# Attention and expert kernel: value sums moved to their rows by DMA and divided there, padded transpositions of maxima and expert weights

## Chip, cores, metric

One core of a Trainium2 chip. The metric is the device time of one execution, in microseconds; lower is better. Engines: PE (TensorE), DVE (VectorE), ACT (ScalarE), POOL (GpSimd), SP (SyncE, which here only issues DMAs).

## The reference

Two blocks over `x` of shape (2, 2048, 256). Block A is windowed attention with keys equal to values; block B is a rotary causal attention with 16 heads of 16, a gate, two of eight experts, and layer norms. Cut to what matters here:

```
x = layernorm(x + windowed_attention(x))                    # "a" steps
q = rope(x) @ Wq.T + bq ; k = rope(x) @ Wk.T + bk ; v = x @ Wv.T + bv      # "r" steps
attn = softmax(causal(q k^T / 4)) ; ctx = attn @ v          # jobs
x1 = LN(x + ctx @ Wo.T + bo) * w + b                        # "d" steps
gates = softmax(x1 @ gate_w.T + gate_b) ; top 2             # "f" steps
moe = sum over experts of gate_e * (x1 @ We.T + be)
x = layernorm(x + LN(x1 + moe) * w + b)                     # "g" steps
```

## The kernel before

The 4096 rows are 32 tiles of 128. Every tile passes the steps `a_*` (window attention), `r_*` (rotation, projections, split of q and k into three bf16 parts that are stored to DRAM and read back stacked) and later `d_*`, `f_*`, `g_*` (output projection, gate and experts, last norms). Between them lie 40 jobs, `JOBS[J] = (s, hg, j0, nj)`: group `s` of four tiles, head group `hg` of four heads, `nj` query tiles. In 24 full jobs `nj` is 4; the first and the last group are halved, 16 half jobs with `nj` = 2.

A job has two passes. First `mx` (PE, L1277) makes scores with queries on partitions and `mr` (DVE, L1006) reduces them to row maxima. `nm_a` to `nm_e` (DVE) negate them and split them into three bf16 parts, `nm_T` (PE, L1287) transposes them, tile by tile, `nm_Tc` (ACT, L900) copies them to `nmT`, and `nm_st` (SP, L749) sends them by four DMAs, one for each head, into three rows of `qs`, where they act as extra contraction rows. Then `st` (PE, L1307) makes the transposed scores with the maxima subtracted, `ex` (ACT, L920) exponentiates into `pbuf`, and `pv` (PE, L1329) sums values: four heads side by side in one bank, each with 16 value rows and a 17th row that holds the denominator. `st` of one job runs beside `mx` of the next.

At the end of a job `o_evac` (ACT) copies the bank to `osb`, `o_T` (PE, L1335) transposes it by tiles, `o_den` (DVE, L1048) inverts the denominators, `o_ctx` (DVE, L1058) multiplies into `ctxn`, which has query rows on partitions. For each tile `d_cT` (PE, L1411) transposes `ctxn` back, `d_cTc` (ACT) copies it, and `d_o` (PE, L1418) projects. In the expert part `f_wts` (DVE) is the row of eight weights, `f_wT` (PE, L1432) transposes it, `f_wTc` copies it, `f_b` (PE, L1435) multiplies it with the eight biases in fp32, and `f_e0` to `f_e3` (PE, L1440) are the experts' products.

All order is fixed beforehand: `plan()` runs a list schedule over the rows of `stage_steps()` and `job_steps()`, each with an engine, a cost in ns, a rank and what it waits for, and every engine executes its part of that one order in sequence. Seven PSUM banks are shared: at most three for `mx`, three for `st`, four for all other steps. A cost that is too low doesn't change the result, only where the engines wait.

Of the kernel before, what the change touches and what calls it, by code (L numbers as in the profile page):

```python
# [8 lines left out]
BF16 = mybir.dt.bfloat16  # L9
# [5 lines left out]
P = 128  # L15
# [7 lines left out]
GT = 4  # L23
# [9 lines left out]

STACKS = ((0, 0, 3, 0), (0, 3, 1, 0), (0, 4, 2, 0), (1, 0, 2, 0), (1, 2, 3, 0), (1, 5, 1, 0))
# [114 lines left out]
def late_count(T):  # L149
# [22 lines left out]
def stage_steps():  # L172
# [67 lines left out]
    for T in range(NT):  # L240
        l, tile = late_prior(T), LATE[T]
        alt = [("st0", NT - 1), ("r_vst", NT - 1), ("pst", NT - 1), ("pv_end", last_job(GB - 1))] if T > TAIL else []
        add("d_load", T, "SP", 450, ("st0", tile), ("d_res", l), *alt)
        add("d_xb", T, "POOL", 700, ("d_load", T), ("load_b2", 0))
        add("d_cT", T, "PE", 215, ("o_ctx", last_job(T // GT, T % GT)), ("d_o", l))
        add("d_cTc", T, "ACT", 280, ("d_cT", T))
        add("d_o", T, "PE", 860, ("d_cTc", T), ("d_aff", l), ("d_xb", T), ("load_moe", 0), ("load_ew", 0))
# [27 lines left out]
        add("f_e1", T, "PE", 1720, ("f_e0", T))  # L275
# [25 lines left out]
def job_steps():  # L301
# [8 lines left out]
    for J in range(NJ):  # L310
# [119 lines left out]
def build(nc, windows, cs, w_qk_t, w_out, in_t, in_b, wo_t, gate_t, exp_t, exp_b, rows, gate_b, out):  # L430
# [6 lines left out]
    with ExitStack() as ctx:  # L437
# [7 lines left out]
        small = sb("small", [P, 350])  # L445
# [96 lines left out]
        cT = [sb("cT", [P, EC, P])[:, :, :], qT[0], halves(room[4]), halves(room[5])]  # L542
        rD = [sb("rD", [P, E])[:, :], xb[0], room[6], room[7]]
# [12 lines left out]
        wT = [x[0:NE, 0:P] for x in accp]  # L556
# [36 lines left out]
        osb_ready, oden_ready = sem("osb_ready"), sem("oden_ready")  # L593

# [35 lines left out]
        CONSTS, MOE_LOADS = 12, 6  # L630
# [4 lines left out]
        def _(sp):  # L635
# [3 lines left out]
            for step in order:  # L639
# [852 lines left out]
```

## Time and profile before

| | |
|---|---|
| median of 3 runs | 1479.54 us (1478.23 to 1481.64) |
| profiled execution, time | 1473.93 us |
| profiled execution, span | 1472.1 us |
| instructions in the profile | 28143 |
| bytes read from HBM, written | 60.71 MB, 25.43 MB |

The span goes from the first to the last instruction of the profiled execution. Busy times are from the same execution; matmuls are pipelined and the end of each is modelled, so that the busy time of a short one contains a tail that the next one overlaps. The chain of work is followed back from the last instruction, at each step to what released it; its pieces go from start to start. A piece of idle time is put down to the semaphore that came last. "PEld" is the loading of weights, which runs beside the matmuls; "SPq" is SP's queue, which issues the DMAs.

### The profile page before, as it was taken

Reading aid. Unit: us, or ns where it says so; the run is one execution under the profiler, and the core shown is the slowest. Engines: PE = TensorE matmul, PEld = TensorE weight load, DVE = VectorE, ACT = ScalarE, POOL = GpSimd, SP = SyncE. Lnnn points to the kernel's source line nnn. Section 1 sums busy time; section 2 is a strip of 40 time slices with the busy share of each in tenths; the row PEclk is TensorE's granted clock in tenths of the full one; section 3 lists DMA queues with packets and bytes.
Section 4 is the critical chain, followed back from the end, with each engine's and each line's share of the span. In section 5 each row is a group of like instructions: output and inputs, shape, how many; then the busy total and the mean of one; then the engine's idle time right before and its main releaser. Section 6 shows DMA issues by size and latency. Waiting matters only on the chain.

```text
span 1472.1 us, 28143 instructions
## 1 busy us (share of the span) xinstructions
PE 1418.3 (96%) x9720; PEld 779.9 (53%) x9720; DVE 1080.3 (73%) x2604; ACT 800.2 (54%) x1707; POOL 427.8 (29%) x704
## 2 busy tenths in 40 slices
PE   8889999999999999999999999999999999999996
PEld 6757745555455545355556555555443345555442
DVE  3755877887788878787546777788777887878645
ACT  3235365555656566665654355555565566665641
POOL 4434423232322222221434433333211111011233
PEclk9999999999999999999999999999999999999998
DMA  3765522230222122010225232223110101111100
GB/s 117 187 172 120 132 56 56 56 88 24 59 56 56 43 61 56 24 45 24 53 68 112 70 87 68 55 57 80 27 48 14 25 24 24 33 31 30 29 26 15
DMA packets 150843, 88.60 MB, mean 60 GB/s; under 512 B 113902, under 2 KB 143862, under 8 KB 150447
## 3 DMA queue, kind: packets, MB, share of 16 engines
q1 hardware_dynamic: 150703, 86.80, 23.6%
q8 instruction: 79, 1.29, 0.4%
q14 instruction: 61, 0.50, 0.1%
HBM read 60.71 MB, written 25.43 MB: 59 GB/s over the span
## 4 chain that ended last, share of the span: by engine, by line
PE 82%; DMA 4%; SPq 4%; DVE 4%; issue 3%; ACT 2%; POOL 1%; POOLq 0%; DVEq 0%; ACTq 0%
PE bank L1329 16%; PE bank L1307 16%; PE bank L1440 14%; PE bank L1277 14%; SPq L749 4%; DMA qs<-eb_nmT 3%; PE bank L1399 3%; PE bank L1377 2%; PE bank L1385 2%; DVE mxs L1006 2%; PE bank L1360 2%; PE bank L1366 1%; PE bank L1405 1%; PE bank L1435 1%; PE bank L1281 1%
## 5 line engine op out<-in xcount | busy, mean ns | idle before, releaser
L1006 DVE TENSOR_REDUCE mxs<-bank 128x1 f32<-128x512 f32 (+3 forms) x1120 | 712.1, 667 | 186.7 <-PE bank L1277 122.0
L920 ACT ACTIVATE pbuf<-bank 128x512 f32<-128x512 f32 (+1 forms) x1112 | 592.2, 592 | 377.8 <-PE bank L1329 203.8
L1307 PE MATMUL bank<-qs,ks 99*128 99x256 bf16 (+3 forms) x1536 | 423.7, 319 | 19.5 <-DMA qs<-eb_nmT 19.3
L1277 PE MATMUL bank<-ks,qs 96*128 96x512 bf16 (+3 forms) x1280 | 421.7, 349 | 2.2 <-DVE mxs L1006 1.7
L1329 PE MATMUL bank<-pbuf,vcur 128*17 128x256 f32 (+3 forms) x3072 | 271.4, 471 | 2.1 <-ACT pbuf L920 1.5
L1307 PEld LDWEIGHTS bank<-qs,ks 99*128 99x128 bf16 x1536 | 140.1, 98 | 199.3 <-issue 112.1
L1440 PE MATMUL bank<-ew,x1T 128*128 128x512 f32 x464 | 220.7, 597 | 0.0
L1277 PEld LDWEIGHTS bank<-ks,qs 96*128 96x128 bf16 x1280 | 123.7, 99 | 126.1 <-issue 52.8
L1329 PEld LDWEIGHTS bank<-pbuf,vcur 128*17 128x17 f32 x3072 | 70.7, 96 | 144.5 <-issue 104.1
L1440 PEld LDWEIGHTS bank<-ew,x1T 128*128 128x128 f32 x464 | 84.2, 190 | 69.0 <-issue 56.9
L900 ACT ACTIVATE etmp<-bank,small 128x256 f32<-128x256 f32 x116 | 48.6, 470 | 78.8 <-PE bank L1440 78.8
L869 POOL TENSOR_TENSOR accp<-accp,etmp 128x256 f32<-128x256 f32 x29 | 21.0, 725 | 223.9 <-ACT etmp L900 223.9
L1281 PE MATMUL bank<-maskb,idb 128*128 128x128 bf16 x384 | 81.1, 220 | 0.0
L865 POOL TENSOR_TENSOR accp<-etmp 128x256 f32<-128x256 f32 x29 | 21.1, 728 | 181.2 <-ACT etmp L900 181.2
L1312 PE MATMUL bank<-idb,maskb 128*128 128x128 bf16 x352 | 73.8, 220 | 0.0
L1203 DVE SCALAR_TENSOR_TENSOR acc<-bank,small,acc 128x256 f32<-128x256 f32 x58 | 28.1, 484 | 54.3 <-PE bank L1440 54.0
L1399 PE MATMUL bank<-rxT,inw 128*128 128x128 f32 x464 | 57.1, 276 | 0.0
L1399 PEld LDWEIGHTS bank<-rxT,inw 128*128 128x128 f32 x464 | 55.4, 192 | 2.0 <-issue 1.0
L815 POOL TENSOR_SCALAR small<-small 128x1 f32<-128x1 f32 x32 | 7.1, 221 | 165.9 <-DVE small L1082 165.9
L841 POOL CAST parts<-qkf 128x512 bf16<-128x512 f32 x28 | 17.3, 618 | 120.2 <-DVE qkf L1098 120.2
L900 ACT ACTIVATE qT<-bank 128x256 f32<-128x256 f32 x59 | 22.7, 384 | 36.8 <-PE bank L1377 19.7
L1281 PEld LDWEIGHTS bank<-maskb,idb 128*128 128x128 bf16 x384 | 37.7, 98 | 8.2 <-issue 3.3
(267 smaller groups left out, 1761.3 us busy)
## 6 DMA issues: line engine op xcount, KB each, us to landing
vcur<-v_scratch SPq DMA_DIRECT2D x92, 136.0 KB, 2.4
parts_scratch<-parts SPq DMA_DIRECT2D x29, 384.0 KB, 3.3
xw<-windows SPq DMA_DIRECT2D x29, 256.0 KB, 2.9
qs<-parts_scratch SPq DMA_DIRECT2D x32, 192.0 KB, 3.4
ks<-parts_scratch SPq DMA_DIRECT2D x32, 192.0 KB, 3.6
ks<-parts_scratch SPq DMA_DIRECT2D x32, 128.0 KB, 2.9
qs<-parts_scratch SPq DMA_DIRECT2D x32, 128.0 KB, 3.5
v_scratch<-vst SPq DMA_DIRECT2D x29, 136.0 KB, 2.1
```

The costliest lines, as they stand in the source:

```text
L749: sp.dma_start(qs5[KR:KR + NPART, place(J) % QRING, j0:j0 + nj, hg * HJ + h, :], nmT[h * NPART:(h + 1) * NPART, 0:nj * P].rearrange("p (j ...
L900: return nc.scalar.activation(o, i, ACT.Copy, scale=scale)
L920: nc.scalar.activation(pbuf[:, u0:u0 + heads, nj * P - cols:nj * P], bk[:, 0:heads * cols].rearrange("p (h t) -> p h t", h=heads), ACT.Exp)\
L1006: v.reduce_max(mxs[:, j * HJ + h:j * HJ + h + heads, c], bk[:, 0:heads * cols].rearrange("p (h t) -> p h t", h=heads), AX_X)\
L1277: last = mm(bk[:, x * cols:(x + 1) * cols].rearrange("p (n t) -> p n t", t=P), qs5[0:KR, pos % QRING, j, head, :], ks5[0:KR, kslot, 0:cols ...
L1281: last = mm(bk[:, x * cols + j * P:x * cols + (j + 1) * P], idb[:, :], maskb[:, :], start=False, stop=True)
L1307: last = mm(bk[:, x * cols:(x + 1) * cols].rearrange("p (n t) -> p n t", t=P), ks5[0:KR + NPART, kslot, kb % GT, head, :], qs5[0:KR + NPAR ...
L1312: last = mm(bk[:, x * cols:x * cols + P], maskb[:, :], idb[:, :], start=False, stop=True)
L1329: last = mm(obank[32 * h:32 * h + DV, r0:r1], vcur[:, kb, h, :], pbuf[:, (kb * HJ + h) % PB, r0:r1], start=kb == 0, stop=kb == nk - 1, til ...
L1360: last = mm(bk[:, co * P:(co + 1) * P], m_sb[:, ci, co * P:(co + 1) * P], xT[e][:, ci, P:2 * P], start=ci == 0, stop=ci == EC - 1)
L1399: last = mm(bk[:, co * P:(co + 1) * P], inw[:, ci, co * P:(co + 1) * P], rxT[e][:, ci, :], start=ci == 0, stop=ci == EC - 1)
L1440: last = mm(bk[:, :], x1T[f][:, c, :], ew[:, c, k * 2 * E:(k + 1) * 2 * E], start=c == 0, stop=c == EC - 1)
```

## The change

Value sums: `o_T`, `o_den`, `o_ctx`, `d_cT` and `d_cTc` are gone. `o_mv` (SP) waits for `osb` and issues five DMAs within SBUF: one for each head, 16 rows of `osb` to the rows of `ctxT` that `d_o` contracts over, and one that copies the four denominator rows to the 16 rows of their head in `oden`. After each second job of a group (`hg` 1 and 3) `o_rec` (DVE) inverts the 128 rows of `oden` and `o_nrm` (POOL) multiplies the part of `ctxT` in place. `d_o` reads `ctxT` directly. `rD` is now the tile `x0b`, so `d_load` waits for `d_aff` of the tile before in place of `d_res`.

Maxima: `nmp` is one 128x128 bf16 tile, zero beyond the parts, transposed by one instruction; `nm_Tc` copies 128 columns; `nm_st` issues one DMA for each tile in place of one for each head.

Expert biases: `f_wp` to `f_ws` (DVE) split the weights into three bf16 parts and lay them out in six slots of a padded tile, which `f_wT` transposes in bf16; `ebp` holds the biases in bf16 parts for the same slots (made once by `w_eb`, and `load_ebp`, six DMAs), and `f_b` is one bf16 product. `f_e0` no longer waits for `f_b`, `f_e1` does.

Cut to its core:

```diff
@@ stage_steps
+    add("w_eb", 0, "DVE", 1200, ("load_moe", 0))
+    add("load_ebp", 0, "SP", 2700, ("w_eb", 0))
...
-        add("d_load", T, "SP", 450, ("st0", tile), ("d_res", l), *alt)
+        add("d_load", T, "SP", 450, ("st0", tile), ("d_aff", l), *alt)
-        add("d_cT", T, "PE", 215, ("o_ctx", last_job(T // GT, T % GT)), ("d_o", l))
-        add("d_cTc", T, "ACT", 280, ("d_cT", T))
-        add("d_o", T, "PE", 860, ("d_cTc", T), ("d_aff", l), ("d_xb", T), ("load_moe", 0), ("load_ew", 0))
+        add("d_o", T, "PE", 860, ("o_nrm", last_job(T // GT, T % GT)), ("d_xb", T), ("load_moe", 0), ("load_ew", 0))
...
+        add("f_wp", T, "DVE", 100, ("f_wts", T), ("f_wT", T - 1))
+        add("f_wq", T, "DVE", 100, ("f_wp", T))
+        add("f_wr", T, "DVE", 100, ("f_wq", T))
+        add("f_ws", T, "DVE", 100, ("f_wr", T))
+        add("f_wT", T, "PE", 100, ("f_ws", T), ("f_b", l), ("f_es", l))
+        add("f_wTc", T, "ACT", 200, ("f_wT", T), ("f_es", l))
+        add("f_b", T, "PE", 200, ("f_wTc", T), ("load_ebp", 0))
-        add("f_e0", T, "PE", 1720, ("f_b", T))
+        add("f_e0", T, "PE", 1720, ("d_x1Tc", T))
@@ job_steps
-        add("nm_T", J, "PE", 420, r - 1, ("nm_e", J))
-        add("nm_Tc", J, "ACT", 495, r - 1, ("nm_T", J), ("nm_st", J - 1))
-        add("nm_st", J, "SP", 1600, r - 1, ("nm_Tc", J))
+        add("nm_T", J, "PE", 100, r - 1, ("nm_e", J))
+        add("nm_Tc", J, "ACT", 200, r - 1, ("nm_T", J), ("nm_st", J - 1))
+        add("nm_st", J, "SP", 1300, r - 1, ("nm_Tc", J))
...
-        add("o_evac", J, "ACT", 495, r + length / 2, ("pv", J, nk - 1), ("o_T", J - 1))
-        add("o_T", J, "PE", 440, r + length / 2, ("o_evac", J), ("d_cT", freed))
-        add("o_den", J, "DVE", 120, r + length / 2, ("o_T", J))
-        add("o_ctx", J, "DVE", 340, r + length / 2, ("o_den", J), ("d_cT", freed))
+        add("o_evac", J, "ACT", 495, r + length / 2, ("pv", J, nk - 1), ("o_mv", J - 1))
+        add("o_mv", J, "SP", 2200, r + length / 2, ("o_evac", J), ("d_o", freed), ("o_nrm", J - 1 - hg % 2))
+        if hg % 2:
+            add("o_rec", J, "DVE", 55 + nj * 133, r + length / 2, ("o_mv", J))
+            add("o_nrm", J, "POOL", 300 + nj * 214, r + length / 2, ("o_rec", J))
@@ SP
+                    for j in range(nj):
+                        sp.dma_start(qs5[KR:KR + NPART, place(J) % QRING, j0 + j, hg * HJ:(hg + 1) * HJ, :],
+                                     nmT[j * NPART * HJ:(j + 1) * NPART * HJ, :]).then_inc(nm_loaded, 16)
+                elif name == "o_mv":
...
+                    sp.wait_ge(osb_ready, J + 1)
...
+                    to = hg % 2 * HJ * DH
                     for h in range(HJ):
+                        sp.dma_start(ctxT[to + h * DH:to + (h + 1) * DH, pos % 2, hg // 2, j0 * P:(j0 + nj) * P],
+                                     osb[32 * h:32 * h + DH, 0:nj * P]).then_inc(ctx_loaded, 16)
+                    sp.dma_start(oden[to:to + HJ * DH, 0:nj * P],
+                                 osb[DH:P:32, 0:nj * P].unsqueeze(1).broadcast_to([HJ, DH, nj * P])).then_inc(ctx_loaded, 16)
@@ POOL
+            for m in (ebp, wpad, nmp):
+                pool.memset(m[:, :], 0.0).then_inc(consts, 1)
+                elif name == "o_nrm":
...
+                    pool.wait_ge(ctx_loaded, 80 * (T + 1))
+                    pool.wait_ge(oden_ready, T // 2 + 1)
+                    pool.tensor_tensor(part, part, oden[:, 0:nj * P], ALU.mult).then_inc(ctx_ready, 1)
@@ DVE
+                    dve.wait_ge(ctx_loaded, 80 * (T + 1))
+                    v.reciprocal(oden[:, 0:nj * P], oden[:, 0:nj * P]).then_inc(oden_ready, 1)
@@ PE
+                    tr(bk[:, 0:P // 2].bitcast(BF16), nmp[:, :], idb[:, :]).then_inc(filled[b], 1)
...
-                    pe.wait_ge(*drain("d_cT", T))
+                    pe.wait_ge(ctx_ready, (last_job(T // GT, T % GT) + 1) // 2)
...
-                    tr(bk[0:NE, 0:P], wts[f], idf[:, :]).then_inc(filled[b], 1)
+                    tr(bk[:, 0:P // 2].bitcast(BF16), wpad[:, :], idb[:, :]).then_inc(filled[b], 1)
...
-                    mm(bk[:, 0:E], wT[f], eb, start=True, stop=True).then_inc(filled[b], 1)
+                    mm(bk[:, 0:E], wT[f], ebp[:, :], start=True, stop=True).then_inc(filled[b], 1)
```

## Rows read from the trace of the kernel before

**Rows 1.** The page, busy us, share of the span and instructions of each engine.
```profile
PE 1418.3 (96%) x9720; PEld 779.9 (53%) x9720; DVE 1080.3 (73%) x2604; ACT 800.2 (54%) x1707; POOL 427.8 (29%) x704
```

**Rows 2.** The page, shares of the chain that ended last, by engine.
```profile
PE 82%; DMA 4%; SPq 4%; DVE 4%; issue 3%; ACT 2%; POOL 1%; POOLq 0%; DVEq 0%; ACTq 0%
```

**Rows 3.** Waits of PE: us in total, times, longest us.
```profile
PE bank L1307 <- DMA qs<-eb_nmT: 19.3, 22, 4.6
...
PE bank L1277 <- DVE mxs L1006: 1.7, 6, 0.5
```

**Rows 4.** Waits of DVE's reductions for PE.
```profile
DVE mxs L1006 <- PE bank L1277: 122.0, 117, 3.6
...
DVE mxs L1006 <- PE bank L1281: 62.9, 60, 4.0
```

**Rows 5.** Chain in order of time, 629 to 660 us: start, us, what.
```profile
631.65 0.32 PE bank L1287 x4
631.97 0.59 PE bank L1335 x4
...
632.77 0.22 PE bank L1411 x2
...
637.51 0.22 PE bank L1277
...
655.50 0.62 PE bank L1435 x2
```

**Rows 6.** Groups by form on DVE: count, busy us, mean ns, idle before.
```profile
L1006 DVE TENSOR_REDUCE mxs<-bank 128x1 f32<-128x512 f32 x896 | 582.0, 682 | 139.9 <-PE bank L1277 112.8 <-PE bank L1281 26.2
...
L1058 DVE TENSOR_TENSOR ctxn<-bank,oden 128x256 f32<-128x256 f32 x24 | 10.0, 415 | 0.0
...
L1048 DVE RECIPROCAL oden<-bank 128x16 f32<-128x16 f32 x24 | 6.0, 252 | 0.5 <-PE bank L1335 0.3
...
L1163 DVE RECIPROCAL small<-small 128x1 f32<-128x1 f32 x32 | 5.0, 158 | 1.2 <-ACT small L972 0.7
...
L1048 DVE RECIPROCAL oden<-bank 128x8 f32<-128x8 f32 x16 | 3.2, 201 | 3.1 <-PE bank L1335 3.1
```

**Rows 7.** Timeline, boundary of two jobs near 1106 us: start, us, instruction, idle.
```profile
1105.38 0.60 ACT L900 ACTIVATE osb<-bank 128x512 f32<-128x512 f32 x1 [0.34 <-PE bank L1329]
1106.57 0.59 ACT L900 ACTIVATE eb_nmT<-bank 12x512 bf16<-12x512 bf16 x1 [0.30 <-PE bank L1287]
1107.19 3.00 SPq L749 DMA_DIRECT2D qs<-eb_nmT  x4
1111.38 0.47 PE L1307 MATMUL bank<-qs,ks 99*128 99x512 bf16 x1 [2.96 <-DMA qs<-eb_nmT]
```

**Rows 8.** Timeline, ACT and SP at a boundary near 632 us.
```profile
630.97 0.58 ACT L900 ACTIVATE osb<-bank 128x512 f32<-128x512 f32 x1
631.00 0.37 SPq L741 DMA_DIRECT2D vcur<-v_scratch  x1
632.92 3.01 SPq L749 DMA_DIRECT2D qs<-eb_nmT  x4
```

**Rows 9.** The page, DMA issues: KB each, median us from issue to landing.
```profile
parts_scratch<-parts SPq DMA_DIRECT2D x29, 384.0 KB, 3.3
...
x0b<-x_scratch SPq DMA_DIRECT2D x29, 128.0 KB, 2.1
```

**Rows 10.** Windows: us, then PE, PEld, DVE, ACT, POOL busy, PEclk, DMA share, GB/s.
```profile
1111.50:1114.90 3.40, 3.40 (x9) 0.99 (x7) 2.30 (x4) 2.28 (x5) 0.00 (x0) 0.50 0.00 0
```

**Rows 11.** Groups by form on ACT: the copy of 128 columns.
```profile
L900 ACT ACTIVATE accp<-bank 8x128 f32<-8x128 f32 x29 | 7.5, 257 | 4.9 <-PE bank L1432 4.9
```

**Rows 12.** Timeline, end of the last job and the projection behind it.
```profile
1422.89 0.38 ACT L900 ACTIVATE osb<-bank 128x256 f32<-128x256 f32 x1 [1.89 <-PE bank L1329]
...
1428.45 1.03 PE L1418 MATMUL bank<-wo,ks 128*128 128x256 f32 x4
```

More of the change, by code:

```diff
@@ L114, in st_last, with tiles_before @@
     return max(i for i, x in enumerate(st_list(J)) if x[0] <= kb)
+def tiles_before(J):
+    return sum(x[3] for x in JOBS[:J])
 def loads_before(J, c):
@@ L159 @@
 EMPTIES = {"w_m": "w_mc", "w_o": "w_oc", "a_xT": "a_xTc", "a_q": "a_qc", "a_s": "a_exp", "a_pT": "a_pTc", "a_y": "a_yc", "a_o": "a_res", "r_rT": "r_rTc",
-           "r_qk": "r_qkf", "r_v": "r_vst", "nm_T": "nm_Tc", "d_cT": "d_cTc", "d_o": "d_res", "d_x1T": "d_x1Tc",
+           "r_qk": "r_qkf", "r_v": "r_vst", "nm_T": "nm_Tc", "d_o": "d_res", "d_x1T": "d_x1Tc",
            "f_g": "f_lg", "f_wT": "f_wTc", "f_b": "f_acc0", "f_e0": "f_e0c", "f_e1": "f_e1c", "f_e2": "f_e2c",
-           "f_e3": "f_e3c", "o_T": "o_ctx", "mx": "mr", "st": "ex"}
+           "f_e3": "f_e3c", "mx": "mr", "st": "ex"}
 EMPTIED_FOR = {reader: filler for filler, reader in EMPTIES.items()}
@@ L467, in build @@
         ew = sb("ew", [P, EC, NE * E])
-        eb_nmT = sb("eb_nmT", [2 * 32, E])
-        eb = eb_nmT[0:NE, :]
-        nmT = eb_nmT[32:32 + NPART * HJ, :].bitcast(BF16)
+        ebp = sb("ebp", [P, E], BF16)
+        wpad = sb("wpad", [P, P], BF16)
         qkb = sb("qkb", [P, 2 * EC])
@@ L541, in build @@
         x0f = [sb("x0f", [P, E])[:, :], xw[0][:, 1, :], room[2], room[3]]
-        cT = [sb("cT", [P, EC, P])[:, :, :], qT[0], halves(room[4]), halves(room[5])]
-        rD = [sb("rD", [P, E])[:, :], xb[0], room[6], room[7]]
+        rD = x0b
         x1 = [sb("x1", [P, E])[:, :], x0[0], room[8], room[9]]
@@ L1019, in _ @@
                     nj = JOBS[T][3]
-                    whole = nm[:, 0:nj * HJ].rearrange("p (j h) -> p j h", j=nj)
-                    rest = nmd[:, 0:nj * HJ].rearrange("p (j h) -> p j h", j=nj)
-                    part = [nmp[:, 0:nj, :, a] for a in range(NPART)]
+                    whole, rest = (x[:, 0:nj * HJ].rearrange("p (j h) -> p j h", j=nj) for x in (nm, nmd))
+                    part = [nmp[:, 0:nj * NPART * HJ].rearrange("p (j a h) -> p j a h", j=nj, a=NPART)[:, :, a, :]
+                            for a in range(NPART)]
                     if name == "nm_b":
+                        if T == 0:
+                            dve.wait_ge(consts, CONSTS)
                         if T:
@@ L1285, in _ @@
                     pe.wait_ge(nmp_ready, T + 1)
-                    for j in range(JOBS[T][3]):
-                        last = tr(bk[0:NPART * HJ, 0:GQ // 2].bitcast(BF16)[:, j * P:(j + 1) * P], nmp[:, j, :, :].rearrange("p h a -> p (h a)"), idb[:, :])
-                    last.then_inc(filled[b], 1)
+                    tr(bk[:, 0:P // 2].bitcast(BF16), nmp[:, :], idb[:, :]).then_inc(filled[b], 1)
                 elif name == "st":
@@ L1331, in _ @@
                     last.then_inc(pv_done, 1)
-                elif name == "o_T":
-                    pe.wait_ge(osb_ready, T + 1)
-                    for j in range(JOBS[T][3]):
-                        last = tr(bk[:, j * P:(j + 1) * P], osb[:, j * P:(j + 1) * P], idf[:, :])
-                    last.then_inc(filled[b], 1)
                 elif name in ("w_m", "w_o"):
@@ L1407, in _ @@
                     last.then_inc(filled[b], 1)
-                elif name == "d_cT":
-                    pe.wait_ge(*drain("o_T", last_job(T // GT, T % GT)))
-                    for c in range(EC):
-                        last = tr(bk[:, c * P:(c + 1) * P], ctxn[:, T % (2 * GT), c * P:(c + 1) * P], idf[:, :])
-                    last.then_inc(filled[b], 1)
                 elif name == "d_o":
```

117 lines of the change are left out of this document (76 added, 41 removed).

## Prediction

> **What bounds the kernel now.** I read the page first, then the waits, the chain in order of time, the groups by form, and the timeline where one job ends and the next begins. PE is busy for 1418.3 of 1472.1 us, DVE for 73% of the span, ACT for 54% [rows 1]. The chain that ended last is 82% PE; DMA, SP's issuing and DVE have 4% each [rows 2]. PE's named waits are few: 19.3 us in 22 waits for the maxima to land in `qs` (`nm_st`), 1.7 us for DVE's reductions [rows 3]. So PE's program is the path, and a microsecond taken from it counts, as long as the other engines deliver in time. Two things say how well they do. DVE idles 1.04 us in the mean before a reduction that waits for PE (122.0 us in 117 times, 62.9 in 60) [rows 4]: it follows PE closely, and a pause of DVE much longer than that is felt by PE. And PE executes an order that `plan()` fixed from the costs written in the kernel; where a real step is longer than its planned one, PE stands at the next instruction that needs it.
>
> The profiled execution has a span of 1472.1 us and a time of 1473.93; the median of the three runs is 1479.54, 0.4% above. I work out a difference on the span and add it to the median.
>
> **Part 1, PE work removed.** A busy mean of a short matmul contains its pipeline's tail, so I price by the chain, which goes from start to start [rows 5]. `o_T`: four transpositions 0.59 us in each of 24 full jobs, half of that in 16 half jobs, 19.0 us. `d_cT`: 0.22 x 32 tiles = 7.0. `nm_T`: four in 0.32 become one in 0.08, 24 x 0.24 + 16 x 0.08 = 7.0. `f_b`: two passes of an 8-row fp32 product in 0.62 become one bf16 product of 256 columns; a bf16 product of 512 columns takes 0.22 there, so I take 0.11 and get 0.51 x 32 = 16.3; at 0.22 it is 12.8. `f_wT` in bf16: one `d_cT` piece takes 0.11, one `nm_T` piece 0.08, 0.03 x 32 = 1. Sum 46.8 to 50.3, I take **-47 us**. The evacuations that go with them (`cT`, the longer copy of `nmT`) relieve ACT, which isn't the bound: nothing.
>
> **Part 2, the division.** Before, DVE inverts 16 numbers per partition (252 ns) or 8 (201) and multiplies from PSUM (415 for a full job) [rows 6]: 24 x 0.667 + 16 x some 0.5 = 24 us. After, `o_rec` inverts denominators that were copied to all 16 rows of a head: 512 columns 12 times, 256 columns 8 times. No row has a wide reciprocal. One column costs 158 ns, 8 cost 201, 16 cost 252: 6.4 ns per column from 8 to 16. A reduction passes 512 columns in 682 ns [rows 6], which is the lower bound, 0.7 us. The slope gives 0.25 + 496 x 0.0064 = 3.4 us, and 1.8 us for 256 columns. I take the slope, as it is the same operation; its two points are strided reads of PSUM, which keeps the lower bound open. DVE's sum: 12 x 3.4 + 8 x 1.8 = 55, plus 4 x 32 `f_wp` to `f_ws` at 0.2 = 26, plus 2 for `w_eb`, less 24: **+59 us of DVE**, 77% busy. That alone wouldn't bound.
>
> The place does. The plan prices `o_rec` at 55 + 133 per tile, 587 ns; with 3.4 us DVE is 2.8 us late, and with it what is queued behind: the reductions `mr` that empty the banks of `mx` (three at most), residuals and sums of the layer norms, the gates. The transfers add to it. `o_mv` is five SP instructions. A plain load takes 0.37 us to issue [rows 8], those of `nm_st`, over three partitions, 0.75 (3.00 for four) [rows 7]. Bounds 1.9 and 3.75 us for five; four of the five span 16 partitions, so I take 2.3. Landing: 2.1 us for 128 KB, 3.3 for 384 KB [rows 9]; the broadcast writes 128 KB from 4 source rows, and I take 3. From the end of `o_evac` to `o_rec` that makes 5.3 us where the plan has 4.1, 1 us late. Full job: 1.0 + 2.8 - 1.04 of slack = 2.8 us of PE idle, 12 times **+34** (bounds: 0 if the reciprocal is cheap and the data are in time; 12 x 4.5 = 54 at the dear issue and landing). Half job: 1.5 + 0.3 late, little above the slack, 8 x 0.5 = **+4** (0 to 12). `o_nrm`, `d_rstd` behind it on POOL and `d_o` on PE stand in the same pause as the reductions, so they aren't priced apart.
>
> What the Trainium skill adds stands apart: "VectorE: DVE Perf Modes", section "First, the fixed hardware budget", says that the reciprocal is an iterative divide with a repeat count of 8. With the 0.96 GHz that the same page of the Trainium skill has under "Specifications" this is, as an estimate, 8.3 ns per column and 4.3 us for 512, and the sum would be 12 x 0.9 = 11 us dearer. The slope of [rows 6] is nearer to it than to one column per cycle.
>
> **Part 3, the maxima.** The copy `nm_Tc` comes down from about 0.6 towards the 257 ns of a 128-column copy [rows 11], `nm_T` by 0.24. `nm_st` of a full job still has four DMAs over three partitions, 3.0 us; that of a half job has two in place of four, 1.5 us less. Where `st` starts some 1.2 us behind the last issue (1107.19 + 3.00 to 1111.38 [rows 7]) this is on the path. By the timeline I count four half jobs of that kind, 4 x 1.8, **-7**, and six full ones with no `o_mv` near, 6 x 0.6, **-4**. In 15 full jobs, though, the sums of the job before are evacuated 0.6 to 2.4 us ahead of `nm_st`: `osb` ends at 1105.98, `nm_st` starts at 1107.19 [rows 7]; 631.55 and 632.92 [rows 8]. There `o_mv` gets into SP's queue first, and `nm_st` and the loads of keys, queries and values stand behind it. 1107.19 becomes 1105.98 + 0.1 + 2.3 = 1108.4, 1.2 us later than now. Part is planned (2200 ns stands in the table) and filled with other work, part isn't: from -0.6 (if `nm_st` goes first) to 2.7, I take 1.0; 15 x 1.0 = **+15**.
>
> **Part 4, the clock.** Before 1111.38 PE stood 2.96 us for `nm_st` [rows 7]; right after, the granted clock was 0.50, 1.2 GHz, for 3.4 us [rows 10]. Half of 3.4, 1.7 us, is lost by such a fall. New pauses of that length will bring some: I take five, **+8** (0 to 15 x 1.7 = 26).
>
> **Part 5, edges.** Start: three more memsets on POOL of the size of those that stand beside the first loads, nothing. Six small DMAs of `ebp` at 0.75 and `w_eb`, while SP issues the loads of the first jobs: 0 to 5, **+2**. End: the last `o_mv`, `o_rec` and `o_nrm` need 0.1 + 2.3 + 2.6 + 1.8 + 0.1 + 0.7 = 7.6 us from 1423.3, so `d_o` starts near 1430.9 and not 1428.45 [rows 12], +2.4; `f_e0`, which no longer waits for `f_b`, gives some back: **+1**. `x0b` serving as `rD` lets `d_load` start some 3 us later, once per tile, and tiles lie 10 us and more apart: nothing. DVE's 26 us of `f_wp` to `f_ws` lie behind `f_wts`, beside expert products; in an engine that is 27% idle they make 0 to 8, **+3**.
>
> **Sum.** -47 + 34 + 4 - 7 - 4 + 15 + 8 + 2 + 1 + 3 = +9 us: 1479.5 + 9 = **1488**.
>
> **Rivals.** (a) The forecast: pauses of DVE and SP eat the gain of PE and more. 0.46; its own range is 1482 to 1502. (b) Faster: PE's removed work counts and the pauses are hidden, by a wide reciprocal near the 0.7 us bound or by work that PE doesn't need soon. Then -47 - 11 + 16 for what remains of the pauses, + 12 for the rest: -30, 1450. For it: PE has 82% of the chain and lost only 1.7 us to DVE. Against: the slope, and 1.04 us of slack. It decides for a pause below some 1.5 us. 0.25. (c) The two cancel, -12 to +2: 1468 to 1482. 0.20. (d) SP's queue bounds every boundary: `nm_st` 2.7 us late in 15 places (+25 against my term) and a fall of the clock at most of them (+18), not all of it together: 1512. It decides when `o_mv` takes 3.75 us to issue. 0.09.
>
> Faster by over 0.2% (3 us, about what a measurement of this kernel tells from no change): (b) and half of (c), 0.35. Within: 0.12. Slower: 0.53. Both signs hold much. The range for 8 in 10 is 1453 to 1510; it leaves out the lower half of (b) and part of (d).
>
> **What would show it.** In the profile after: a reciprocal of 128x512 near 3.4 us (0.7 turns me to (b), 4.3 to the skill's estimate); PE's waits for DVE's `mxs` up from 1.7 to 20 us or more, with PE's idle before `d_o` beside them; the wait for `qs` above 19.3; four DMAs of `o_mv` at 0.4 and one at 0.75 to issue; a mean granted clock under the present one. I am wrong in kind if PE's idle time grows by less than 40 us, and wrong in size if the new order of `plan()`, which the trace of before can't show, puts `o_rec` where DVE has room.

## The result and the profile after

The change makes the kernel slower than every case I had written down: 1604.47 us (1604.04 to 1606.6) against 1479.23, a ratio of 1.0847, 95% interval 1.0828 to 1.0866, +125 us. I had forecast 1488 and a range to 1510. The profiled execution has a span of 1602.5 us, 130.4 above the one before.

The page of the changed kernel, busy time of each engine and the line of the granted clock in 40 slices, answers to [rows 1]:

```profile
PE 1433.8 (89%) x9408; PEld 766.4 (48%) x9408; DVE 1138.2 (71%) x2676; ACT 776.8 (48%) x1675; POOL 452.4 (28%) x727
...
PEclk9988999999999989999999999999998999999997
```

PE has 312 instructions fewer and is yet busy for 15.5 us longer, while its share fell from 96% to 89%; DVE's fell from 73% to 71% though it has 58 us more to do. Idle time has come in on both engines, and PE's work itself has slowed down. PE's waits by what they waited for (us in total, times, longest), answer to [rows 3]:

```profile
PE bank L1373 <- DMA qs<-nmT: 46.8, 17, 6.1
PE bank L1474 <- POOL ctxT L896: 32.1, 6, 8.7
PE bank L1354 <- DVE nmp L1084: 15.2, 4, 7.2
PE bank L1345 <- DVE mxs L1052: 11.5, 11, 5.7
PE bank L1373 <- DVE mxs L1052: 7.0, 14, 1.8
```

L1373 is `st`, L1474 `d_o`, L1354 `nm_T`, L1345 `mx`. The wait for the maxima to land grew from 19.3 to 46.8 us. `d_o` now waits for `o_nrm`, `nm_T` for the split maxima, `mx` for the reductions: 64 us more than before, in few and long pieces. Next, DVE's own waits, answer to [rows 4]. Those of its reductions for PE grew by 13 us in all; the new row behind them is its stand at `o_rec`:

```profile
DVE mxs L1052 <- PE bank L1345: 123.4, 111, 3.2
DVE mxs L1052 <- PE bank L1349: 74.7, 64, 3.4
DVE oden L1095 <- DMA oden<-osb: 57.7, 19, 6.0
```

The groups by form (busy us, mean ns, idle before), answer to [rows 6] and [rows 11]: the wide reciprocal, what POOL waits for behind it, two of the four steps of the padded weights (290 to 166 ns, 25.7 us in all four), and the short copy of the maxima.

```profile
L1095 DVE RECIPROCAL oden<-oden 128x512 f32<-128x512 f32 x12 | 40.2, 3353 | 37.8 <-DMA oden<-osb 37.8
L896 POOL TENSOR_TENSOR ctxT<-ctxT,oden 128x512 f32<-128x512 f32 x12 | 15.2, 1265 | 89.0 <-DVE oden L1095 89.0
L1095 DVE RECIPROCAL oden<-oden 128x256 f32<-128x256 f32 x8 | 14.0, 1752 | 20.0 <-DMA oden<-osb 20.0
...
L1245 DVE TENSOR_TENSOR small<-small,wpad 128x8 f32<-128x8 f32 x32 | 9.3, 290 | 0.2
...
L1249 DVE TENSOR_TENSOR wpad<-small,wpad 128x8 bf16<-128x8 f32 x32 | 5.3, 166 | 0.1
...
L948 ACT ACTIVATE nmT<-bank 48x128 bf16<-48x128 bf16 x24 | 6.4, 266 | 19.5 <-PE bank L1354 19.4
```

One boundary shows how the pieces hang together. Timeline of the changed kernel, end of job 27 (start, us, instruction, idle before), answer to [rows 7]; it is put together from the rows of five engines, in order of time:

```profile
1101.80 0.60 ACT L948 ACTIVATE osb<-bank 128x512 f32<-128x512 f32 x1 [1.17 <-PE bank L1395]
...
1103.78 2.48 SPq L788 DMA_DIRECT2D ctxT<-osb  x4
1106.31 0.64 SPq L790 DMA_DIRECT2D oden<-osb  x1
1107.06 1.59 SPq L749 DMA_DIRECT2D qs<-parts_scratch  x2
...
1109.66 3.07 SPq L774 DMA_DIRECT2D qs<-nmT  x4
1110.77 3.35 DVE L1095 RECIPROCAL oden<-oden 128x512 f32<-128x512 f32 x1 [3.23 <-DMA oden<-osb]
1114.26 1.27 POOL L896 TENSOR_TENSOR ctxT<-ctxT,oden 128x512 f32<-128x512 f32 x1 [9.84 <-DVE oden L1095]
1115.67 2.04 PE L1474 MATMUL bank<-wo,ctxT 128*128 128x256 f32 x4 [6.00 <-POOL ctxT L896]
1117.51 0.63 PE L1373 MATMUL bank<-qs,ks 99*128 99x512 bf16 x1
```

`osb` is full at 1102.4, `o_mv` starts 1.4 us later and takes SP's queue 3.2 us, its last transfer lands 3.8 us after that. DVE stands 3.23 us at `o_rec` and then divides for 3.35; POOL multiplies for 1.27; PE stands 6.00 us before `d_o`. `nm_st` starts at 1109.66, behind two loads and a store that stand before it in SP's order. From the full `osb` to `d_o` it is 13.3 us. The windows of the same boundary (us, busy of PE, PEld, DVE, ACT, POOL, granted clock, DMA), and of two other places, answer to [rows 10]:

```profile
1106.00:1112.80 6.80, 3.67 (x28) 3.06 (x26) 3.51 (x6) 0.54 (x2) 0.00 (x0) 1.00 0.33 88
1112.90:1119.60 6.70, 3.93 (x9) 2.64 (x10) 5.89 (x13) 1.73 (x4) 4.74 (x5) 0.50 0.12 40
1119.70:1126.00 6.30, 6.05 (x37) 2.16 (x36) 4.59 (x11) 4.14 (x9) 1.48 (x3) 1.00 0.41 107
1215.30:1228.80 13.50, 8.15 (x24) 1.84 (x28) 11.36 (x18) 4.67 (x8) 1.95 (x2) 0.50 0.08 24
```

While PE stands, the granted clock falls to 0.50 (1.2 GHz) at 1112.8 and stays there until 1119.6, over `d_o` (four products in 2.04 us, where four took 1.03 at the full clock [rows 12]) and the first `st` of the next job. The fourth row is 13.5 us at half clock, with PE busy for 8.15 of them; they begin within a pause of 6.1 (the longest of the wait for `qs`). The chain of this profile covers only some 40% of the span, so its shares, unlike [rows 2], tell nothing.

For the whole execution I laid the trace's records of the granted clock against PE's idle pieces. The time lost to the clock is half of what PE works at 0.50; what it idles there is counted once, as idle. The idle time includes the 4 us before PE's first instruction.

| | span | PE idle | at half clock (spells) | of it PE idle | lost to the clock | rest |
|---|---|---|---|---|---|---|
| before | 1472.1 | 43.0 | 26.1 (5) | 3.7 | 11.2 | 1418.0 |
| after | 1602.5 | 157.8 | 175.7 (24) | 44.3 | 65.7 | 1379.1 |

The 130.4 us are +114.8 of idle, +54.5 of slow clock and -38.9 of work removed. The rest is the span less the idle time and less what the clock lost: what the kernel would take if PE never stood and the clock never fell. As a remainder it holds the errors of the others: the six kernels of the table of mended prices have the same instructions and rests from 1372.8 to 1389.8, so a difference of rests is good to some 17 us and no better. Spans are of the profiled executions; that of before is a short one (1473.93 us of time against medians of 1477.6 to 1479.5, a mean granted clock of 0.991 where the other executions have 0.984 to 0.992), so differences of spans and of medians differ by up to 5 us, and part of the +54.5 belongs to that choice.

The end, answer to [rows 12]: timeline of the last job and the projection behind it.

```profile
1556.93 0.38 ACT L948 ACTIVATE osb<-bank 128x256 f32<-128x256 f32 x1 [0.96 <-PE bank L1395]
...
1562.85 1.75 DVE L1095 RECIPROCAL oden<-oden 128x256 f32<-128x256 f32 x1 [5.96 <-DMA oden<-osb]
...
1565.61 3.75 PE L1474 MATMUL bank<-wo,ctxT 128*128 128x256 f32 x8 [8.74 <-POOL ctxT L896]
```

### The profile page after: what moved, and what is told of

The parts are those of the page before. It is cut to its first block and busy times, and to the rows that moved or that the text cites. A ratio compares the mean times of both kernels' runs of the same rounds, so it can differ in the third digit from the quotient of the medians.

```text
span 1602.5 us, 27748 instructions
## 1 busy us (share of the span) xinstructions
PE 1433.8 (89%) x9408; PEld 766.4 (48%) x9408; DVE 1138.2 (71%) x2676; ACT 776.8 (48%) x1675; POOL 452.4 (28%) x727
## 5 line engine op out<-in xcount | busy, mean ns | idle before, releaser
L1373 PE MATMUL bank<-qs,ks 99*128 99x256 bf16 (+3 forms) x1536 | 441.3, 332 | 58.4 <-DMA qs<-nmT 46.8
L1345 PE MATMUL bank<-ks,qs 96*128 96x512 bf16 (+3 forms) x1280 | 436.1, 361 | 14.5 <-DVE mxs L1052 11.5
L1373 PEld LDWEIGHTS bank<-qs,ks 99*128 99x128 bf16 x1536 | 143.3, 100 | 258.4 <-issue 150.3
L1345 PEld LDWEIGHTS bank<-ks,qs 96*128 96x128 bf16 x1280 | 126.2, 101 | 154.2 <-issue 56.8
L1095 DVE RECIPROCAL oden<-oden 128x512 f32<-128x512 f32 (+1 forms) x20 | 54.2, 2712 | 57.7 <-DMA oden<-osb 57.7
L1474 PE MATMUL bank<-wo,ctxT 128*128 128x256 f32 x128 | 40.8, 451 | 32.1 <-POOL ctxT L896 32.1
L901 POOL TENSOR_TENSOR x0b<-x0b,rowv 128x256 f32<-128x256 f32 x29 | 21.1, 728 | 149.9 <-DMA x0b<-x_scratch 148.6
L896 POOL TENSOR_TENSOR ctxT<-ctxT,oden 128x512 f32<-128x512 f32 (+1 forms) x20 | 21.0, 1052 | 137.4 <-DVE oden L1095 137.4
```

The lines of the kernel that those rows point to most:

```text
L1095: v.reciprocal(oden[:, 0:nj * P], oden[:, 0:nj * P]).then_inc(oden_ready, 1)
L1345: last = mm(bk[:, x * cols:(x + 1) * cols].rearrange("p (n t) -> p n t", t=P), qs5[0:KR, pos % QRING, j, head, :], ks5[0:KR, kslot, 0:cols ...
L1373: last = mm(bk[:, x * cols:(x + 1) * cols].rearrange("p (n t) -> p n t", t=P), ks5[0:KR + NPART, kslot, kb % GT, head, :], qs5[0:KR + NPAR ...
L1474: last = mm(bk[:, 0:E], ctxT[:, T // GT % 2, c, T % GT * P:(T % GT + 1) * P], wo[:, c, :], start=c == 0, stop=c == EC - 1)
```

## The experiments

My theory after the result: neither the instructions nor the transfers are what costs 125 us, but the order that `plan()` makes from prices that are too low. `o_mv` stands there at 2200 ns and with the default size of 4 KB for its landing, `o_rec` at 55 + 133 per tile, `nm_st` at 1300. The rivals: the reciprocal's length as such; the queue of SP as such; the clock, started by any pause. Times of before in the tables are those of runs on the same chip.

### Each half alone

The pads alone: `nm_T`, `nm_st`, `f_wp` to `f_b` and `ebp` as in the change, the value sums as before. The value sums alone: `o_mv`, `o_rec`, `o_nrm`, `d_o` as in the change, the maxima and the biases as before.

> The padded maxima and the bf16 expert biases alone; value sums go through PE's two transpositions as before. Theory A (the time is lost in the value sums' transfers and the wide reciprocal): about 25 us faster than the kernel before, 1445 to 1465, as PE loses 0.51 x 32 for the biases and 7 us of maxima transpositions, and nm_st of half jobs gets shorter. Rival B (the small DVE steps f_wp to f_ws and the new order cost as well): 1475 to 1500.

> The value sums by transfers alone; maxima and biases as before. Theory A: all of the loss and more is here, 1610 to 1640. Rival B (loss shared by both parts, or only through their meeting): 1540 to 1590.

| | us | before | ratio (95%) | idle | lost to the clock | rest |
|---|---|---|---|---|---|---|
| pads alone | 1464.58 | 1478.24 | 0.9917 (0.9888 to 0.9947) | 46.8 | 15.7 | 1400.2 |
| value sums alone | 1625.59 | 1478.24 | 1.1009 (1.0973 to 1.1045) | 152.3 | 72.4 | 1397.8 |

The loss lies in the value sums: +147 us, and the pads take 13.7 off. The sum, +134, is near the +125 of both together. Both numbers are those of theory A, though its "about 25 us" for the pads was nearly twice what came. The rests put PE's removed work at -17.8 for the pads and -20.2 for the value sums, with the error named above.

PE's waits in the kernel with the value sums alone:

```profile
PE bank L1313 <- DMA qs<-eb_nmT: 36.4, 16, 4.0
PE bank L1428 <- DVE small L1197: 20.4, 7, 9.2
PE bank L1283 <- DVE mxs L1024: 18.3, 15, 6.0
```

The same stall of DVE at `o_rec` comes out at other places of PE's program: here L1428, the transposition of the gate weights (`f_wT`), which in the changed kernel hardly waits. Which step is the victim is a matter of the order; that there is one isn't.

### The reciprocal without its time

The changed kernel with a multiplication by 1.0 in the reciprocal's place; the division of the value sums is left out.

```diff
-                    v.reciprocal(oden[:, 0:nj * P], oden[:, 0:nj * P]).then_inc(oden_ready, 1)
+                    v.tensor_scalar(oden[:, 0:nj * P], oden[:, 0:nj * P], 1.0, None, ALU.mult).then_inc(oden_ready, 1)
```

> The changed kernel with a multiplication by 1.0 in place of the reciprocal of oden, so the division is left out; order and all waits as in the changed kernel. It takes 12 x 2.7 + 8 x 1.3 = 43 us from DVE. Theory A1 (the length of the reciprocal is the main cost): DVE's pauses shrink from some 6 us to 3.5, falls of the clock become few, 1604 goes to 1500 to 1540. Rival A2 (DVE standing for the landing of oden, SP's queue ahead of nm_st, and the clock falls behind these are the main cost): 1560 to 1590, with PE's wait for qs still over 40 us.

1559.85 us, ratio 1.0556 (1.0514 to 1.0598): 44.6 us below the changed kernel. 81 us of the 125 stay. The time lies at the very edge of theory A2, 20 us from A1. The groups by form and the waits of this kernel:

```profile
L1095 DVE TENSOR_SCALAR oden<-oden 128x512 f32<-128x512 f32 x12 | 5.4, 448 | 38.5 <-DMA oden<-osb 38.5
...
PE bank L1373 <- DMA qs<-nmT: 46.8, 17, 5.5
PE bank L1474 <- POOL ctxT L896: 19.9, 6, 7.3
PE bank L1354 <- DVE nmp L1084: 8.4, 4, 3.9
```

DVE works 46.1 us less at this place and PE idles 34.6 us less, at `d_o`, `nm_T` and `mx` above all, and loses 6 us less to the clock. DVE's stand for the transfer (38.5 us in the full jobs, 37.8 before) and PE's wait for `qs` don't move.

### The plan told the truth

Five kernels have the changed kernel's instructions and other prices. One has all of these, the others one or two:

```diff
-          "load_moe": 300, "load_ew": 2048, "st0": 128, "vstore": 136, "pst": 384, "d_load": 128, "g_load": 128,
+          "load_moe": 300, "o_mv": 400, "load_ew": 2048, "st0": 128, "vstore": 136, "pst": 384, "d_load": 128, "g_load": 128,
...
-        add("nm_st", J, "SP", 1300, r - 1, ("nm_Tc", J))
+        add("nm_st", J, "SP", nj * 750, r - 1, ("nm_Tc", J))
...
-        add("o_mv", J, "SP", 2200, r + length / 2, ("o_evac", J), ("d_o", freed), ("o_nrm", J - 1 - hg % 2))
+        add("o_mv", J, "SP", 3150, r + length / 2, ("o_evac", J), ("d_o", freed), ("o_nrm", J - 1 - hg % 2))
...
-            add("o_rec", J, "DVE", 55 + nj * 133, r + length / 2, ("o_mv", J))
+            add("o_rec", J, "DVE", 55 + nj * 825, r + length / 2, ("o_mv", J))
```

400 KB is no size that is moved; at the plan's 5 ns per KB it is 2.0 us more of landing. `plan()` lets transfers pass one after another, so this number also sets back the transfers that it places behind `o_mv`.

> The changed kernel with four costs in the plan set to what its trace shows (o_mv 3150 and a landing longer by 2 us, nm_st 750 per tile, o_rec 55 + 825 per tile); the work is the same, only the order moves. Theory C (the loss comes from a plan that doesn't know the real lengths): 1604 goes to 1480 to 1530 and the granted clock comes back to 0.98 or more. Rival D (the lengths themselves hurt, no order hides them): 1560 to 1610.

> The changed kernel with only o_rec's cost set right in the plan (55 + 825 per tile in place of 133). C1: 20 to 40 us back, 1565 to 1585. C2: 60 or more, under 1545.

> The changed kernel with only o_mv's cost set right in the plan (3150 and a landing longer by 2 us). Of the 115 us that all four costs gave back: theory C1 (the steps wait for each other in one pause, and knowing where it begins is worth most) 60 to 90 us, 1515 to 1545. Rival C2 (the reciprocal's price is what matters): under 40 us, 1565 or more.

> The changed kernel with one number of the plan altered: the issuing of o_mv is priced at 3150 ns in place of 2200. The pair of prices for o_mv (issue 3150 and 400 KB for its landing) had brought 1604 to 1519 us. Theory I (the SP queue: nm_st and the loads stand behind an o_mv that takes 0.95 us longer than planned): most of the 85 us come from this number, 1535 to 1560 us here, and the wait for qs falls from 46.8 to near 23 us while DVE's wait for oden stays near 50. Theory L (the landing, which the plan has at zero size, so that DVE stands at o_rec): this number gives back little, 1580 to 1600 us, and DVE's wait for oden stays above 50 us.

> The changed kernel with the other number alone: o_mv enters the plan as a transfer of 400 KB, so that o_rec is placed behind its landing; its issuing stays at 2200 ns. Theory I: 1575 to 1600 us, the wait for qs stays above 40 us. Theory L: 1520 to 1545 us, DVE's wait for oden falls from 57.7 to under 20 us and PE's waits for the reductions' mxs below 8 us.

| prices mended | us | before | ratio (95%) | idle | lost to the clock | rest |
|---|---|---|---|---|---|---|
| none | 1604.47 | 1479.23 | 1.0847 (1.0828 to 1.0866) | 157.8 | 65.7 | 1379.1 |
| `o_rec` | 1573.68 | 1479.52 | 1.0644 (1.0601 to 1.0688) | 130.6 | 64.0 | 1381.1 |
| `o_mv`, issue | 1575.28 | 1477.55 | 1.0664 (1.0637 to 1.0691) | 134.1 | 61.0 | 1377.3 |
| `o_mv`, landing | 1560.82 | 1477.55 | 1.0566 (1.0534 to 1.0597) | 119.1 | 69.6 | 1372.8 |
| `o_mv`, both | 1518.88 | 1479.52 | 1.0274 (1.0237 to 1.031) | 94.0 | 33.8 | 1387.0 |
| all | 1489.55 | 1478.24 | 1.0081 (1.0053 to 1.011) | 71.6 | 29.0 | 1389.8 |

115 of the 125 us come back with four numbers changed and not one instruction, as theory C had it. This is the finding of the case. Its parts: 85.6 us by the pair for `o_mv` and 30.8 by the price of `o_rec`, both as C1 had them; the price of `nm_st` wasn't tried alone in this kernel. The pair isn't one of its halves: issue alone gives 29, landing alone 44, together less than both at once. Neither of theories I and L has its number. The landing is what makes DVE stand: its wait for `oden` falls from 57.7 to 18.9 us with the landing priced, to 41.1 with the issue. But the wait for `qs` moves with neither alone (45.0 and 44.2), only with both (22.9), and the clock's loss likewise; with `o_rec` priced alone it rises to 58.0. And PE's waits for the reductions, which L had below 8 us, are 31.8 with the landing priced: what leaves one place comes out at another. Waits with the landing priced alone:

```profile
PE bank L1373 <- DMA qs<-nmT: 44.2, 20, 4.7
PE bank L1373 <- DVE mxs L1052: 22.0, 15, 3.6
PE bank L1345 <- DVE mxs L1052: 9.8, 18, 3.4
```

Waits with all prices mended:

```profile
PE bank L1373 <- DMA qs<-nmT: 18.0, 16, 3.5
PE bank L1474 <- POOL ctxT L896: 5.9, 3, 4.8
...
DVE oden L1095 <- DMA oden<-osb: 11.3, 7, 4.5
```

And the boundary of job 27 in that kernel, rows of SP, DVE, POOL and PE in order of time, with its window:

```profile
1014.64 2.49 SPq L788 DMA_DIRECT2D ctxT<-osb  x4
1017.17 0.64 SPq L790 DMA_DIRECT2D oden<-osb  x1
...
1018.34 3.54 SPq L774 DMA_DIRECT2D qs<-nmT  x4
1021.53 3.35 DVE L1095 RECIPROCAL oden<-oden 128x512 f32<-128x512 f32 x1
...
1025.03 1.27 POOL L896 TENSOR_TENSOR ctxT<-ctxT,oden 128x512 f32<-128x512 f32 x1 [1.29 <-DVE oden L1095]
1026.45 1.10 PE L1474 MATMUL bank<-wo,ctxT 128*128 128x256 f32 x4
```

```profile
1013.00:1030.00 17.00, 16.33 (x89) 10.53 (x87) 16.53 (x45) 7.76 (x19) 6.32 (x8) 1.00 0.56 145
```

The transfers take as long as in the changed kernel (3.2 us to issue, 3.7 until `o_rec`), the reciprocal takes 3.35 us, the multiplication 1.27. PE and DVE hardly stand: DVE is busy for 16.5 of 17 us, PE for 16.3, the clock is 1.00.

One rival isn't excluded by a run of its own: that some of the gain is due to another order as such and not to the right one. No order from prices altered at random was run. Against it stands that each of the five price changes here made the kernel faster, and the two of `nm_st` below didn't make theirs slower.

### The clock by itself

The changed kernel with additional products whose result is overwritten: 10 before the first `st` of each job and 20 before `d_o` of seven tiles, so that PE works where it would stand.

```diff
+                        for _ in range(10):
+                            mm(bk[:, :].rearrange("p (h t) -> p h t", h=HJ), maskb[:, :],
+                               idb[:, :].unsqueeze(1).broadcast_to([P, HJ, P]), start=True, stop=True)
```

> The changed kernel, its plan and waits as they are, with extra products on PE ahead of two of its waits: 10 of 512 columns (2.2 us) before each first st of a job, 20 (4.4 us) before d_o of seven tiles, written to a bank that the real products overwrite. They add work and take the idle time away. Theory E (each pause costs twice, by itself and by the 3.4 to 7 us of half clock behind it; 178 us at half clock in the changed kernel, 28 before): half-clock time falls under 100 us and the time to 1545 to 1580, although PE has more to do. Rival F (the clock's falls come from elsewhere or cost little): 1604 to 1650, as 40 x 2.2 us of work are added where the wait is shorter.

1635.56 us, ratio 1.1063 (1.1029 to 1.1097), 31 us slower. Idle is 96.3 (-61.5), lost to the clock 44.1 (-21.6), the rest 1493.3 (+114.2, the 540 products). The groups of the added products:

```profile
L1367 PE MATMUL bank<-idb,maskb 128*128 128x512 bf16 x400 | 95.0, 385 | 0.5 <-DVE mxs L1052 0.5
...
L1477 PE MATMUL bank<-idb,maskb 128*128 128x512 bf16 x140 | 37.7, 433 | 4.4 <-DVE mxs L1052 4.4
```

The time is that of rival F and not of theory E (1545 to 1580). F's reason, that the falls come from elsewhere, isn't borne out: the time at half clock fell from 175.7 to 100.1 us. Of the 114.2 us added, 61.5 took the place of standing; the other 53 made the kernel longer and cost more than the clock gave back. The run agrees with the share that I give the clock (21.6 us of slow clock go with 61.5 us of idle, 0.35 per us; with all prices mended it was 36.7 with 86.2, 0.43) and doesn't prove it: it isn't a run in which the clock alone was changed, and there is none.

### What is left over

The kernel with all prices mended, 1490 us, stands above the pads alone. Three more runs ask what its value sums still cost, and how much of the pads' gain is a price as well.

```diff
-            add("o_rec", J, "DVE", 55 + nj * 825, r + length / 2, ("o_mv", J))
+            for k in range(nj):
+                add(f"o_rec{k}", J, "DVE", 60 + 825, r + length / 2, ("o_mv", J), *[(f"o_rec{k - 1}", J)] * (k > 0))
...
-                    v.reciprocal(oden[:, 0:nj * P], oden[:, 0:nj * P]).then_inc(oden_ready, 1)
+                    k = int(name[5:])
+                    v.reciprocal(oden[:, k * P:(k + 1) * P], oden[:, k * P:(k + 1) * P]).then_inc(oden_ready, 1)
```

> The kernel with the plan priced by the trace (1490 us), and o_rec cut into pieces of 128 columns, four of some 0.9 us in place of one of 3.35, each a step of its own, so that reductions can stand between them. Theory P (what is left of the loss is the unbroken pause of DVE): PE's gaps fall from 71.6 to near 60 us and the time to 1470 to 1480. Theory Q (the plan already puts the reciprocal where DVE has room, and what is left is the work and the order): 1485 to 1497, DVE's work only 3 us more.

1493.0 us, 1.0122 (1.0092 to 1.0153): no gain, as theory Q had it; the 3 us more lie within the two intervals. Idle is 75.9 (71.6 unsplit), and the 64 pieces take DVE 59.7 us where the 20 wide ones took 54.1. In this kernel, a pause that the plan knows needn't be cut.

> The kernel with the plan priced by the trace (1490 us), with the reciprocal of the denominators replaced by a multiplication by 1.0 (the division is left out), and priced as what it takes: 55 + 75 ns per tile in place of 55 + 825. It removes some 46 us of DVE's work from a kernel whose plan knows it. The pads with nm_st at its price stand at 1462.5 without the transfers, 27 us lower. Theory R (what the transfer route still costs is the wide reciprocal): 1462 to 1474 us. Theory S (it is the transfers: SP's 3.1 us in front of nm_st and their landing before d_o): 1480 to 1490 us, the wait for qs stays near 18 us.

1482.09 us, 1.0026 (1.001 to 1.0042): 7.5 us below the 1489.55 of the kernel with its reciprocal, as theory S had it (the ratios differ by 0.0055, and their intervals just don't meet). The same edit took 44.6 us off where the plan had the price wrong. So 46 us of DVE's work cost 45 us unplanned, and 44 us of it cost 7 planned. Some 20 of the 27 us over the pads with `nm_st` priced (below) stay, and lie with the transfers or the order around them: idle is 70.9 against 44.1, the clock loses 21.4 against 12.4, the wait for `qs` is 15.2 against 3.6, and `d_o` waits 10.2. Which of SP's queue and the landing holds them is open.

```diff
-        add("nm_st", J, "SP", 1600, r - 1, ("nm_Tc", J))
+        add("nm_st", J, "SP", 3000, r - 1, ("nm_Tc", J))
```

This edit is of the kernel before; in the pads alone the same price became `nj * 750`.

> The kernel before the change with nothing altered but the plan's price of nm_st, 3000 ns (what the trace shows for its four DMAs) in place of 1600. Theory W (the wait for qs, 19.3 us and the falls of the clock behind it, is a price that the plan has wrong, in the kernel before as well): 1465 to 1474 us, the wait for qs below 6 us. Theory V (the order before was balanced around that wait, and another order gives elsewhere what it saves): within 3 us of 1479.5. It also tells what of the best version's gain (1462.5 for pads with nm_st at its price) the padding itself holds.

> The padded maxima and bf16 biases alone, with nm_st's cost in the plan at 750 per tile, as measured. If a right cost helps wherever it was wrong: 5 to 15 us under pads_only's 1464.6. If nm_st's price mattered only behind o_mv: within 3 us of it.

The kernel before with `nm_st` priced: 1469.91 us, 0.9949 (0.9933 to 0.9965). The pads with it: 1462.45 us, 0.9894 (0.987 to 0.9917), the lowest time of this study and faster than both kernels. Waits of the kernel before with the price mended (19.3, 22, 4.6 unmended [rows 3]):

```profile
PE bank L1307 <- DMA qs<-eb_nmT: 2.6, 1, 2.6
```

16.7 us of wait are gone and 7.6 of time are gained: idle fell by 8.5 us, since other waits took part of it, and the clock loses 5.4 more in the profiled executions, 16.6 in place of 11.2. The last number is no finding: the profiled execution of before has a granted clock of 0.991, but over all executions the medians of both kernels are 0.987 to 0.988. Priced pads are another 7 to 8 us faster (1469.9 to 1462.5 on two chips; the ratios are 0.0055 apart).

Theory W held for the kernel before. For the pads the expectation failed: `nm_st`'s price was to bring them 5 to 15 us under 1464.58, and it brought 2.1, with intervals of the ratios that overlap (0.9888 to 0.9947, 0.987 to 0.9917), although the wait for `qs` fell from 11.4 to 3.6 us. So about half of what the pads gain over the kernel before could be had without them, by one right price; their own share is the 7 to 8 us.

## Why the prediction was wrong

The sign was right and the likeliest case, (a), named the right mechanism. The size was off by 116 us. My sum had idle +48, clock +8, work -47; the trace has +115, +54, -39.

The step that failed is the price of the pauses, in two terms. In a full job I had DVE 1.0 + 2.8 = 3.8 us late at `o_rec`; it is 3.15 + 2.8 = 6 us late, because the transfers of `o_mv` take longer to issue and to land than I took. And of the clock I took five falls of 1.7 us, 8 in all; there were 24 spells for 5, and 54 us. Behind both lies that I charged each underpriced step at its own place: the runs show that right prices for the same instructions give 115 us back. Of the 67 us of idle that I missed, 26 are waits for `mxs`, `nmp` and `ctxT`, 23 the wait for `qs`, and some 17 many small waits of PE elsewhere (23 us more than before, the longest 4.1), for which I had 6.

**PE's work removed.** Taken at -47, the rests give -39. The chain's pieces were too high, by 20% as taken and by some 30% as summed: they give 24 us for the pads and 26 for the value sums, the rests 18 and 20. As rests are good to 17 us only, this is not settled.

**The reciprocal.** Taken at 3.4 and 1.8 us by the slope of two short forms [rows 6]: 3.353 and 1.752. From 256 to 512 columns it is 6.25 ns per column. The 8.3 ns and 4.3 us that I had estimated from the Trainium skill's repeat count of 8 ("VectorE: DVE Perf Modes", "First, the fixed hardware budget") are too dear by over a quarter for this form; the measurement decides. A multiplication by 1.0 of the same form took 0.45 us.

**`o_mv` and its landing: the step that failed first.** I took 2.3 us to issue and 3 to land, 5.3 from the end of `o_evac` to `o_rec`, where the plan has 4.1, and called that 1.0 us late. Four DMAs of 16 partitions take 2.48 us and not 1.5 (0.37 was a load from DRAM [rows 8]), the broadcast 0.64; the landing takes 3.7 to 3.9 us in full jobs. In job 31, where SP was free, it makes 6.9 us, 2.8 over the plan; in job 27, where SP had another step first, 8.4. The issue was inside the bounds that I had written (1.9 to 3.75), and I took the lower part of them; the landing was beyond my dearest row, 3.3, though that row counts from the start of an issue and my term from its end.

**Full jobs, 12 x 2.8 = +34, and half jobs, +4.** DVE stood 37.8 us before the full `o_rec`, 3.15 each, and then ran 2.8 us over its price, so it was 6 us late and not 3.8. The terms that stand for it, waits of PE for `mxs`, `nmp` and `ctxT`, came to 64 us in place of 38. A late `o_rec` stops `d_o` at one job (27, above) and `nm_T` at another; timeline at 842 us, where `o_rec` stands in DVE's order before the last two steps of the maxima:

```profile
842.74 3.35 DVE L1095 RECIPROCAL oden<-oden 128x512 f32<-128x512 f32 x1 [4.98 <-DMA oden<-osb]
846.01 0.11 DVE L1081 CAST nmp<-nmd 128x16 bf16<-128x16 f32 x1
846.16 0.18 DVE L1084 TENSOR_TENSOR nmp<-nmd,nmp 128x16 bf16<-128x16 f32 x1
...
846.48 0.27 PE L1354 MATMUL bank<-idb,nmp 128*128 128x128 bf16 x1 [7.21 <-DVE nmp L1084]
```

DVE is away for 4.98 + 3.35 = 8.3 us, 7.7 more than planned, and PE stands 7.2. The slack is 0.5 us here where I had 1.04, and the way of reckoning holds at this job; the pause was twice what I had.

**`nm_st` behind `o_mv`, +15, and the pads' gain at `qs`, -11.** The two are +4 together; the wait for `qs` grew by 27.5 us. The right price for `o_mv` takes that wait from 46.8 to 22.9, so most of the growth comes from an order made for a shorter `o_mv`. Rival (d), "SP's queue bounds every boundary", had the place but 1512 as its price, and it was a share of the loss and no case apart.

**The clock, +8: the largest miss in proportion.** I took five falls of 1.7 us. There were 24 spells against five, and the loss grew by 54 us. Nineteen more falls of 1.7 us would be 32; the rest is that most spells lasted longer than the one of 3.4 us from which I had the price [rows 10]: 15 of the 24 lasted 6.8 us, and two 14 and 17. The trace of before already had two of 6.8 among its five. One row was made a unit price. And the number of falls should have followed from my own sum: 12 pauses of full jobs and 15 late `nm_st` are not five.

**The edges** held in kind: the end of the last `o_evac` to `d_o` takes from 1557.31 to 1565.61, 8.3 us where I had 7.6, but the clock stands at 0.50 from 1560.0 to 1577.1 and again for the last 8.4 us, 25.5 us where the end of before had 12.4, which I hadn't priced. The pads' steps at 0.17 to 0.29 us are the 26 us that I had.

**The range.** Each of these terms had a dear end written beside it: 54 for 34, 12 for 4, 15 x 2.7 = 40 for 15, 26 for 8. They are 20 + 8 + 25 + 18 = 71 us above what I took: 1559, not yet the 1604 measured, but far beyond my range. I treated them as independent and let the range end at 1510. They don't come independently: a dearer `o_mv` makes DVE late, `nm_st` late, and the pauses long enough for the clock at once. And the sentence that the new order of `plan()` could put `o_rec` "where DVE has room" should have been turned round: the order with wrong prices is where it hasn't. The plan's prices for the new steps stood in the diff, and my own rows gave three of them as too low (4.1 us for 5.3 of `o_mv`, 0.6 for 3.4 of `o_rec`, 1.3 for 3.0 of `nm_st`); I charged each difference at its own step and job only.

## What to carry to other kernels

When every engine runs a fixed order made from a table of costs, a new step is only as good as its row in the table: first price it from the trace (issue, landing, duration), then judge the idea. A long step that is planned costs a fraction of its length, one that isn't can cost all of it, the clock behind it included (7 against 45 us here, for some 45 us of DVE's work). When several unknown costs share a queue or a consumer, their dear ends come together, and a range has to add them.

## What the runs showed of the hardware

A transfer within SBUF of 16 partitions by 512 or 256 columns takes SP 0.58 us to issue in the median (0.61 in the mean) and one that spreads four rows to 64 takes 0.64, where a load from DRAM takes 0.37. The copies of the maxima (`qs<-nmT`) take 0.72 in the median and up to 1.8. The spread of 128 KB from four rows is usable 3.7 to 3.9 us after the end of its issue, a half job's of 64 KB 2.4 to 3.0 where DVE stood waiting for it. Counted from the start of the issue, as in [rows 9], the former is 4.4 to 4.6, where a plain 128 KB took 2.1.

In the changed kernel 22 of the 24 spells at 1.2 GHz began in or just behind a pause of PE of 1.8 to 8.7 us, and lasted 3.4 to 17 us, in a kernel in which PE is busy for nine tenths of the time. Over the kernels with the whole change the time lost so went from 24 to 70 us, and it doesn't follow idle time alone: with the landing priced PE idles 39 us less and loses 4 us more to the clock.
